# Second layer of a fused two-layer transformer on Trainium2: scores, transposed scores and the transposes of the maxima moved by a chunk

## The reference

```python
q = x @ Wq.T; k, v = split(x @ Wkv.T)             # 16 heads of 8
sim = where(causal, q @ k.T * 8 ** -0.5, -max)
m = stop_gradient(max(sim, axis=-1)); e = exp(sim - m)
attention = (e @ v) / (sum(e) + 1e-8) @ Wo.T
ffn = sum over 8 experts of (silu(x @ Wg) * (x @ Wu)) @ Wd   # 128 -> 512 -> 128
```

## Time and profile before

| | |
|---|---|
| three runs | 1544.48 to 1552.41 us, median 1550.32 us |
| profiled execution | 1551.97 us, span 1550.3 us |
| PE busy | 1333.5 us, 86% of the span |
| DVE busy | 1037.0 us, 67% |
| ACT busy | 827.8 us, 53% |
| POOL busy | 683.0 us, 44% |

### The profile page before, as it was taken

The page is one execution under the profiler, slowest core; times in us unless marked ns, Lnnn a source line. Parts: engine busy times, 40 slices in busy tenths (PEclk is TensorE's granted clock), DMA queues, the critical chain, the costliest instruction groups (busy, mean ns, idle before and its releaser), DMA issues. The chain is left out here.

```text
span 1550.3 us, 23118 instructions
## 1 busy us (share of the span) xinstructions
PE 1333.5 (86%) x8104; PEld 758.2 (49%) x8104; DVE 1037.0 (67%) x2444; ACT 827.8 (53%) x1236; POOL 683.0 (44%) x789
## 2 busy tenths in 40 slices
PE   4777878787777778469999999999999999999987
PEld 2333433333333333236656666656566656665645
DVE  5555656565656554147878878788787878787843
ACT  2444555554555555236666565656665656565640
POOL 4132333333333423336565555465655655555540
PEclk8677969696968878669999999999999999999997
DMA  5122222222222312241001001010010100000003
GB/s 180 43 71 66 84 89 78 91 84 84 84 84 84 102 33 70 63 123 44 30 25 51 29 27 48 25 49 25 29 45 29 45 30 25 29 25 18 15 23 109
DMA packets 54256, 88.61 MB, mean 57 GB/s; under 512 B 9943, under 2 KB 20700, under 8 KB 54142
## 3 DMA queue, kind: packets, MB, share of 16 engines
q1 hardware_dynamic: 52990, 86.61, 17.9%
q10 hardware_dynamic: 1152, 0.52, 0.1%
HBM read 41.69 MB, written 44.31 MB: 55 GB/s over the span
## 5 line engine op out<-in xcount | busy, mean ns | idle before, releaser
L1146 POOL TENSOR_TENSOR a_h_lo<-a_h,a_h_hi 128x512 fp32r<-128x512 f32 x256 | 329.5, 1287 | 160.4 <-ACT a_h_hi L1193 159.5
L648 DVE TENSOR_REDUCE l_mx<-bank_pair 128x2 f32<-128x1024 f32 (+3 forms) x256 | 204.4, 820 | 224.3 <-PE bank_pair L891 224.3
L130 PE MATMUL bank_pair<-st 24*128 24x512 f32 (+3 forms) x1024 | 218.0, 416 | 92.5 <-DVE l_mx L648 64.2
L1255 DVE SCALAR_TENSOR_TENSOR a_h<-a_h,bank_pair 128x512 f32<-128x512 f32 x256 | 175.3, 685 | 140.2 <-ACT a_h L1189 140.2
L189 POOL TENSOR_SCALAR_AFFINE_SELECT l_E<-l_E 128x256 f32<-128x256 f32 (+1 forms) x192 | 98.7, 514 | 327.8 <-ACT l_E L737 327.8
L165 DVE CUSTOM_DVE_ANT_0 bank_pair<-bank_pair,mask 128x512 f32<-128x512 f32 (+3 forms) x512 | 237.8, 516 | 7.0 <-PE bank_pair L130 6.8
L737 ACT ACTIVATE l_E<-bank_pair 128x1024 f32<-128x1024 f32 (+1 forms) x192 | 167.4, 879 | 122.6 <-PE bank_pair L137 122.5
L1200 ACT ACTIVATE a_E<-bank_pair 128x1024 f32<-128x1024 f32 (+1 forms) x192 | 169.8, 884 | 114.0 <-PE bank_pair L137 114.0
L1193 ACT ACTIVATE a_h_hi<-a_h 128x512 fp32r<-128x512 f32 x256 | 161.6, 631 | 128.8 <-DVE a_h L1261 125.3
L130 PEld LDWEIGHTS bank_pair<-st 24*128 24x128 f32 x1024 | 109.6, 201 | 231.4 <-issue 142.9
L1261 DVE TENSOR_TENSOR a_h<-a_h,bank 128x512 f32<-128x512 f32 x256 | 175.9, 687 | 27.1 <-DVE a_h L1255 0.5
(11 more groups left out here) (128 smaller groups left out, 2174.6 us busy)
## 6 DMA issues: line engine op xcount, KB each, us to landing
st<-stack_d SPq DMA_DIRECT2D x256, 96.0 KB
stack_d<-l_q_k_hi SPq DMA_DIRECT2D x64, 256.0 KB, 3.0
stack_d<-l_q_k_lo SPq DMA_DIRECT2D x32, 256.0 KB, 3.2
o_d<-l_O SPq DMA_DIRECT2D x32, 256.0 KB, 2.1
o_d<-a_O SPq DMA_DIRECT2D x32, 256.0 KB, 2.0
l_at<-o_d SPq DMA_DIRECT2D x8, 256.0 KB, 3.3
l_share<-rden_d SPq DMA_DIRECT2D x8, 256.0 KB, 3.1
a_wst<-wg_in SPq DMA_DIRECT2D x8, 256.0 KB, 3.1
```

Of the source, the lines that this page charges most:

```text
L130: return nc.tensor.matmul(bank[:, col:col + w], st[rows, 0, bass.ts(t, P)], st[rows, 1, 0:w], start=first, stop=last)
L648: ins = nc.vector.tensor_reduce(out, pair[:, :, col:col + width(kb)], AX.X, ALU.max)
L1146: nc.gpsimd.tensor_tensor(h_lo[:, q % RH, :], h[:, q % RH, :], h_hi[:, q % RH, :].bitcast(F32), ALU.subtract).then_inc(h_lo_ready, 1)
L1255: nc.vector.scalar_tensor_tensor(hq, hq, 1.0, g_bank[:, :], ALU.add, ALU.mult).then_inc(silu_ready, 1)
```

## The change

The three hand-written orders of PE, ACT and POOL are moved; DVE and the transfers keep theirs. Transposed piece m stands in chunk c = m instead of m + 1, together with the scores piece of the same size. So the exponential of piece m and its `causal` stand a chunk earlier too. The maxima's transposes move from c7 (behind `gate_up`) to the end of c6 (behind `down`), and ACT's copy of them moves from c7, ahead of `hi`, to c6, behind `hi`.

```diff
@@ POOL
-                    if odd and n < 3:
-                        causal(g, 3 + n)
-                    if not odd and n > 0:
-                        causal(g, n - 1)
+                    if NC * odd + n < UNITS_A_QUAD:
+                        causal(g, NC * odd + n)
                     lo(NC * i + n)
@@ ACT
                     tanh(NC * i + n)
-                    if odd and n < 3:
-                        exp(g, 3 + n)
-                    if not odd and n > 0:
-                        exp(g, n - 1)
-                    if odd and n == NC - 1 and g + 1 < QUADS:
+                    if NC * odd + n < UNITS_A_QUAD:
+                        exp(g, NC * odd + n)
+                    hi(NC * i + n)
+                    if odd and n == NC - 2 and g + 1 < QUADS:
                         copy_mrow(g + 1)
-                    hi(NC * i + n)
@@ PE
                     gate_up(i, n)
-                    if odd and n == 3 and more:
-                        maxima_rows(g + 1)
-                    c = NC * odd + n
-                    scores_and_keys(g, c if c < UNITS_A_QUAD else None, c - 1 if 0 < c <= UNITS_A_QUAD else None)
+                    if NC * odd + n < UNITS_A_QUAD:
+                        scores_and_keys(g, NC * odd + n, NC * odd + n)
@@
                     if NC * i + n >= LAG:
                         down(NC * i + n - LAG)
+                    if odd and n == NC - 2 and more:
+                        maxima_rows(g + 1)
```

## The result

| | before | changed |
|---|---|---|
| median of the runs | 1551.37 us (4 runs, 1544.48 to 1554.47) | 1577.85 us (4 runs, 1577.52 to 1580.61) |
| ratio, 95% interval | | 1.0181 [1.0144, 1.0217] |
| span of the profiled execution | 1550.3 us | 1578.9 us |
| first to last gate of the second layer | 815.52 us | 842.21 us |

The changed kernel is slower by 1.8%, 26.5 us. The spans differ by 28.6 us, of which 26.7 lie between the first and the last gate of the second layer.

A forecast was written before the change was run, and what follows sets the result against it. PE was taken to pace c0 to c2, DVE and ACT c2 to c7. Terms 14.9 + 7.0 + 0.9 = 22.8 us gave 1574.8 on the profiled execution, 1573 on the median (chance 0.56); range 1556 to 1586.

The forecast's parts named there:

- Copy of the maxima ahead of the tanh: In c7, the copy delays tanh, silu and next gate by 0.48 us; 31 copies cost 14.9 us, bounds 12 to 19.
- Negations behind POOL: In c6: `lo` holds the first negation, worth 0; in seven split quads the second waits for the split, 7.0 us.
- The maxima's DMAs: They land in time for c0's scores with 0.24 us to spare; first and last quad together cost 0.9 us.
- What PE gets back: PE's work shrinks 0.89 us per quad in c2, c3, c5 and c6, booked at 0 since DVE and ACT pace there.
- the window of c3: PE's time in c3 from first scores to down matmul, forecast to fall from 0.77 to 0.44 us.
- the trace agrees: Claim that 0.77 us in c3 against 0.44 in c2 bears out that matmuls in the same row group queue.
- the negation escapes: Rival, chance 0.15: the first negation precedes `lo`, the second is held 0.23 us less, no loss behind the split; 1559 us.
- PE's saving shows in part or as a whole: Two rivals on c7's gate: 0.45 us a quad reaches it, some 1552 us, chance 0.11; all 0.89, 1538 us, 0.06.
- the late maxima: Rival, chance 0.09: the maxima's DMAs take 0.6 us longer, c0 waits 0.36 a quad, +11, so 1584 us.
- the granted clock: Rival, chance 0.03: PE's clock falls to 1.2 GHz in c7's longer gap, giving over 1600 us.

## Why the prediction was right, and where it was off

The forecast of 22.8 us met 26.7 in the stage. Term by term:

- **Copy of the maxima ahead of the tanh, 14.9 us: right.** 0.47 a quad instead of 0.48; the copy alone gives 14.7 us.
- **Negations behind POOL, 0 in plain quads and 7.0 in the seven: right.** `lo` and the first negation came 0.07 apart, as worked out (864.86 and 864.93), the first negation took over the standstill, and only behind the split the second has one of its own; taking the split away gives 7.25 us back. The Trainium skill (GPSIMD Engine Reference, Specifications) says that the two engines share their SBUF interfaces, with contention for DVE instructions with two SBUF inputs or in a 2-port performance mode. The trace agrees for the second negation, which has two such inputs. The first has one and was held as long (1.26 us); in which mode it ran no trace here shows.
- **The maxima's DMAs, 0.9: right in kind.** PE waited for them in the first quad alone, 0.56 us. In the last quad, which has no maxima to prepare, c0 took 4.55 instead of 4.13, and the whole of it 0.17 more. Left to land one ACT instruction later, they cost 0.6 in every quad, which bears out that there was hardly anything to spare.
- **What PE gets back, booked at 0: this is the step that was off**, by -0.15 us a quad. Two of its parts failed.

  The first part: the window of c3 was to be 0.44 and was 0.71. The prediction put the 0.77 of before down to scores and transposed scores in the same rows of the array, and took its 0.33 above 0.44 as PE's saving. But most of that was the wait of the pair's second scores for the maxima that DVE took of the piece before. In the kernel before they start at 848.36, 0.23 behind the first ones and 0.57 behind the start of the last of those maxima (847.79); in the changed kernel at 856.63, 0.29 behind the first and 0.58 behind the start of the maxima (856.05). The add behind the maxima removes the wait, and 0.44 appears. The rows of the array are left with some 0.1 of the 0.33, an estimate (0.77 - 0.23 - 0.44). They do show in the kernel before: there the transposed scores start at 848.48, 0.34 behind the scores in the same rows, and in the changed kernel, in other rows, within 0.01 of the second scores. So the prediction's "the trace agrees", by 0.77 against 0.44, holds in kind and not by the size.

  The second part: the prediction followed the order of ACT only around c7. In c3 the exponential is one of 1024 columns now, 1.03 us; begun as late as 857.21, it is done only behind the end of c3's product (857.91), and holds the hi, the copy of the values' product and the tanh behind it by 0.14. In 24 quads this is 3.6 us. The run with the add behind the maxima gives it back in c2 to c7 (14.69); the run with the hi ahead of the exponential shows the hi's delay directly, and at five times the size that this chain is paced by ACT.

The sum of what was found: 14.6 + 7.0 + 0.6 + 3.6, 7 x 0.04 in the split quads and 0.2 in the last, 26.3 of the 26.7. The rest is not placed.

Of the rivals, that the negation escapes, and that PE's saving shows in part or as a whole, were refuted by the same rows (c2 to c7 grew by 0.16); the late maxima are real but one instruction away; the granted clock of the changed kernel stayed at 1.00.

## What to carry to other kernels

Before an instruction is moved ahead, list on each engine what then stands between a released input and the next link of the chain: one copy of 0.48 us ahead of a tanh was 0.9% of this kernel, though the engine was busy for half of the time. Look for instructions whose median is far above their minimum (176 and 1218 ns): what they stand behind is often on another engine, and one wait that puts the long instruction behind the short one took 21.7 us off the stage, 1.4% of the kernel's time. And don't undo a change that lost before its costs have been taken apart: this order was worth 6 us once three neighbours were put right.

## What the runs showed of the hardware

- A DVE instruction of 16 elements, with SBUF operands alone, stood still until the subtraction that POOL was running ended: 0.18 us became 1.22 with two SBUF inputs and 1.26 with one. Where POOL went straight on to a second subtraction, that one ran first, and the DVE instruction issued 0.11 us behind its start waited it out too (919.15, 1.19 us). The silus and products, which also read PSUM, kept 0.67 to 0.69 us beside POOL's work.
- In the run with the transposed scores alone PE stands idle for 1.84 us in each of the seven split quads, and in five of them the granted clock then fell:

```profile
924.43:926.27 1.84, 0.00 (x0) 0.00 (x0) 1.78 (x2) 0.00 (x0) 1.16 (x1) 1.00 0.00 0
926.27:929.91 3.64, 3.64 (x14) 2.63 (x14) 2.67 (x4) 1.90 (x4) 2.16 (x2) 0.68 0.00 0
929.91:931.50 1.59, 1.59 (x6) 1.31 (x5) 0.00 (x0) 0.62 (x2) 1.44 (x2) 0.66 0.04 10
931.50:935.00 3.50, 3.50 (x27) 1.43 (x26) 2.69 (x6) 1.95 (x3) 1.44 (x3) 1.00 0.40 119
```

  The matmuls start 0.43 us apart at 929.48 and 929.91 and 0.23 apart from 931.11 on: part of the stretch was at 1.2 GHz, the rest at 2.4. The changed kernel idles there as well, but has the maxima's transposes in the gap, and kept 1.00 in its split quads. So did the run with the copy behind the tanh again, which differs from this one in one thing only, that the transposes stand at the end of c6: PE stood idle for 1.25 us ahead of them, and c7 took 2.66 in all seven. So in these executions the transposes' place kept the clock up; why it stayed up in two of the seven quads without them is open.
- In the profiled execution with the outputs in c1 the record has a granted clock of 0.95 all through the stage, neither of the two levels. PE's own stretch was longer by 0.10 us in 8.05, less than the clock's 5%, and the median distance of two gate matmuls was 0.232 us as in the changed kernel. The other three executions of that kernel have the mean clock of the rest (0.892 to 0.897 over the whole, against 0.854). The cause was not sought.
- The maxima's two DMAs take 2.59 us from issue to the scores that waited for them (870.52 to 873.11).
